# One of four units of a routed layer multiplied without its layer norm, the norm applied to its outputs

## Time and profile before

| what | value |
|---|---|
| median of 3 runs | 748.06 us (747.79 to 748.12) |
| the profiled execution's own time | 747.98 us |
| its span | 745.7 us |
| PE / DVE / ACT / POOL busy | 737.4 / 509.2 / 337.6 / 42.8 us |
| instructions | 10192 |
| DMA | 117.32 MB, mean 157 GB/s |

### The profile page before, as it was taken

One profiled execution on the slowest core, in us unless ns is written; L12 is line 12 of the kernel. 1 busy time (PEld: TensorE's weight loads), 2 busy tenths in 40 slices (PEclk: granted clock), 3 DMA queues, 4 the chain that ended last, 5 costly groups with the idle time before them and its releaser, 6 DMA issues.

```text
span 745.7 us, 10192 instructions
## 1 busy us (share of the span) xinstructions
PE 737.4 (99%) x4269; PEld 611.9 (82%) x4269; DVE 509.2 (68%) x490; ACT 337.6 (45%) x427; POOL 42.8 (6%) x51
## 2 busy tenths in 40 slices
PE   7999999999999999999999999999999999999997
PEld 7988887888888888888788888888888888888885
DVE  6899987876767586379989997664633644355522
ACT  5868874746673325242844364234233241333221
POOL 3302203010302000000000000000000000000000
PEclk9999999999999999999999999999999999999999
DMA  9644872547252543667596721170037003200140
GB/s 358 273 171 170 280 262 94 212 160 261 102 184 99 184 142 113 240 212 254 170 388 189 293 87 74 73 306 1 1 141 286 25 1 142 113 2 0 51 180 3
DMA packets 28077, 117.32 MB, mean 157 GB/s; under 512 B 4160, under 2 KB 4352, under 8 KB 20992
## 3 DMA queue, kind: packets, MB, share of 16 engines
q1 hardware_dynamic: 18784, 99.88, 37.1%
q10 hardware_dynamic: 9248, 16.80, 6.0%
HBM read 95.60 MB, written 37.77 MB: 179 GB/s over the span
## 4 chain that ended last, share of the span: by engine, by line
PE 87%; DVE 8%; DMA 2%; issue 1%; ACT 1%; POOL 0%; SPq 0%; DVEq 0%; ACTq 0%
PE main L939 28%; PE main L941 27%; PE main L940 27%; PE lgp L1002 1%; DMA x5f<-xT 1%; PE lgp L1015 1%; PE spare L1015 1%; DVE x5f L1097 1%; DVE x4f L1097 1%; DVE x2f L1097 1%; DVE x7f L1097 1%; DMA wh6f<-x 1%; PE main L1026 0%; PE lgp L955 0%; DVE x3r L1097 0%
## 5 line engine op out<-in xcount | busy, mean ns | idle before, releaser
L1097 DVE TENSOR_TENSOR s<-s,main 128x512 f32<-128x512 f32 x72 | 48.6, 682 | 71.6 <-PE main L941 71.6
L1097 DVE TENSOR_TENSOR u<-u,main 128x512 f32<-128x512 f32 x36 | 24.5, 684 | 41.9 <-PE main L941 41.9
L793 ACT ACTIVATE u<-u 128x512 f32<-128x512 f32 x32 | 20.0, 631 | 56.7 <-DVE u L1097 56.7
L770 ACT ACTIVATE s<-main 128x512 f32<-128x512 f32 x36 | 20.8, 595 | 53.0 <-PE main L941 22.3
L793 ACT ACTIVATE s<-s 128x512 f32<-128x512 f32 x32 | 20.0, 630 | 52.2 <-DVE s L1097 52.1
L793 ACT ACTIVATE rows<-rows 128x512 f32<-128x512 f32 x16 | 10.1, 632 | 64.1 <-DVE rows L1097 64.1
L1097 DVE TENSOR_TENSOR u<-s,main 128x512 f32<-128x512 f32 x32 | 21.6, 684 | 22.5 <-PE main L941 22.4
L1097 DVE TENSOR_TENSOR rows<-s,main 128x512 f32<-128x512 f32 x16 | 11.0, 688 | 30.2 <-PE main L941 30.2
L723 ACT ACTIVATE rows<-rows,nm 128x1024 f32<-128x1024 f32 x23 | 26.6, 1154 | 0.8
L721 ACT ACTIVATE rows<-rows 128x1024 f32<-128x1024 f32 x24 | 25.2, 1049 | 1.9 <-DMA rows<-x 1.2
L940 PE MATMUL main<-x7r,wh2r 128*128 128x512 f32 x48 | 18.7, 389 | 0.0
(11 more groups left out here) (691 smaller groups left out, 2424.2 us busy)
## 6 DMA issues: line engine op xcount, KB each, us to landing
out<-x SPq DMA_DIRECT2D x31, 512.0 KB, 10.5
rows<-x SPq DMA_DIRECT2D x26, 512.0 KB, 4.4
H_d<-u ACTq DMA_DIRECT2D x32, 256.0 KB, 3.5
H_d<-s ACTq DMA_DIRECT2D x16, 256.0 KB, 4.9
rows<-xh_d SPq DMA_DIRECT2D x16, 256.0 KB, 5.5
w2f<-w2T SPq DMA_DIRECT2D x2, 2048.0 KB, 10.1
wl6f<-wB SPq DMA_DIRECT2D x3, 1024.0 KB, 8.2
wl4f<-wB SPq DMA_DIRECT2D x3, 1024.0 KB, 6.5
```

What stands on the lines that cost most here:

```text
L770: eng.activation(s1[:, j, :], bk, ACT.Copy).then_inc(s_pa, 1)
L793: eng.activation(c, c, ACT.Silu).then_inc(s_sl, 1)
L1097: return eng.tensor_tensor(o, a, b, op)
```

## The change

**Unit 0** now takes batch 1 (`BATCH = (1, 0, 2, 3)`; batch 0 is unit 1, `RAW = 1`) and multiplies it as it is. Its blocks are loaded transposed: a in 4 pieces of 256 KB and c in 2 of 512 KB, each in turn with a piece of its weights. No row is normalized or transposed on PE, and `warm` runs 18 transposes once. The silu of unit 0 is left out, so that its plain outputs go to DRAM; its logits are raw too.

**Row jobs.** 40 jobs go through the two row buffers on ACT (`row_sums`): the rows of units 1, 2, 3, of unit 0, and of w1 (a sum only). They reach into unit 3, and row 11 of before (the fourth job) is ACT's. SP's order within a position is now: load of the row, then `stats_out`, then `stats_back`, then `save`. The saves of the normalized batch for unit 4 move to unit 1's blocks: at (6,1) and (6,3) of unit 0 and (0,2) and (1,0) of unit 1, and three sums of unit 1 and its last low part wait for them.

**Last unit.** The second layer takes the units in the order 1, 2, 3, 0. In unit 8 each block gets `fold` (DVE: mean times the sum of the w1 row, less the value, times the deviation) and `activated` (ACT: silu with scale -1). Its blocks are loaded at (4,0), (4,1), (6,0), (6,1) of unit 7. The logits of unit 0 are put right in unit 4 by six DVE operations ahead of `two_greatest`; PE gives the sums of wr with one matmul.

The core of the diff (much of it left out):

```diff
+BATCH = (1, 0, 2, 3)
+RAW = 1
+SOURCE = {L2: 1, L2 + 1: 2, L2 + 2: 3, L2 + 3: 0}
+FOLDED = tuple(n for n in SOURCE if SOURCE[n] < RAW)
+JOBS = [(u, r) for u in (1, 2, 3, 0) for r in range(KT)] + [("w1", r) for r in range(KT)]
+PIECES = {"a": 4, "c": 2}
...
+        job_at = {at: q for q, at in enumerate(
+            [(0, *at) for at in ((2, 1), (2, 3), (3, 0), (3, 1), (3, 3), (4, 0), (4, 2), (5, 0), (6, 0), (6, 2))]
...
+        turned_at = {(0, 4, 0): 2, (0, 6, 0): 3, (1, 1, 3): 4, (1, 5, 1): 5, (2, 1, 3): 6, (2, 5, 1): 7, (3, 1, 3): 0,
+                     (3, 3, 3): 1}
+        back_at = {(0, 4, 1): (1, 0), (0, 6, 1): (1, 1), (1, 2, 0): (2, 0), (1, 5, 2): (2, 1), (2, 2, 0): (3, 0),
+                   (2, 5, 2): (3, 1)}
+        save_at = {(0, 6, 1): "a", (0, 6, 3): "c", (1, 0, 2): "b", (1, 1, 0): "d"}
...
+            def row(q):
+                if q >= 2:
+                    job_done(on, q - 2)
+                of, r = JOBS[q]
+                r0 = r * P if of == "w1" else BATCH[of] * SEQ + r * P
+                eng.dma_start(job_buf(q), (w1 if of == "w1" else x)[r0:r0 + P, :]).then_inc(s_row[q % 2], 16)
...
-            for r in (0, 1):
-                row(r)
-            for k in (0, 1):
-                first_weights(k)
...
+            for b in "ac":
+                for k in range(PIECES[b]):
+                    first_block(b, k)
+                    first_weights(b, k)
             weights(0, 5, 2, 1)
+            load(0, "b")
+            load(0, "d")
+            eng.dma_start(cst[:, :], small).then_inc(s_cst, 16)
             weights(0, 4, 2, 2)
+            row(0)
+            row(1)
...
+                if (n, p, j) in job_at:
+                    q = job_at[(n, p, j)] + 2
+                    if q < len(JOBS):
+                        row(q)
+                if (n, p, j) in turned_at:
+                    stats_out(turned_at[(n, p, j)])
+                if (n, p, j) in back_at:
+                    stats_back(*back_at[(n, p, j)])
+                if (n, p, j) in save_at:
+                    save(save_at[(n, p, j)])
...
+            def first_product(k):
+                part_in(on, "a", k)
...
+                    ins = three(main[bank[(0, 0, j)]][:, :], wh[:, k, js], wl[:, k, js], xh[:, k, :], xl[:, k, :],
+                                k == 0, False)
...
-            warm(spare, 29)
-            on.wait_ge(s_id, 2)
-            turn(0)
-            turn(1)
-            warm(main[0], 14)
...
+            warm(spare, 18)
+            for k in range(4):
+                first_product(k)
...
                     if at == (1, 3):
                         for b in "acbd":
                             logits(0, b)
+                        on.wait_ge(s_one, 1)
+                        on.wait_ge(s_sw, 1)
+                        eng.matmul(wr_sums, ones, wrs[:, :], start=True, stop=True).then_inc(s_wm, 1)
...
+            def fold(n, b):
+                kh, h = BLK[b]
+                v = xf(n, b)
+                loaded_in(on, n, b)
+                on.wait_ge(s_bc[1], 16 * BACK[1][(n, h)])
+                job_done(on, len(JOBS) - 1)
+                mean, rstd = bcs[1][:, 0, :], bcs[1][:, 1, :].unsqueeze(1).to_broadcast([P, 4, HT])
+                for j in range(4):
+                    o = 4 * kh + j
+                    ins = eng.scalar_tensor_tensor(v[:, j, :], mean, ws[:, o:o + 1], v[:, j, :], ALU.mult, ALU.subtract)
+                link(ins)
+                tt(v, v, rstd, ALU.mult).then_inc(s_fd, 1)
...
+            def logits_normalized():
...
+                for s in range(2 * RAW):
+                    of = L[:, 4 * s:4 * s + 4, :]
+                    mean, rstd = (mvu[:, s, 4 * e:4 * e + 4].unsqueeze(2).to_broadcast([P, 4, E]) for e in range(2))
+                    part_ = rest[:, 4 * s:4 * s + 4, :]
+                    link(tt(part_, mean, wr_sums.unsqueeze(1).to_broadcast([P, 4, E]), ALU.mult))
+                    link(tt(of, of, part_, ALU.subtract))
+                    link(tt(of, of, rstd, ALU.mult))
...
                 if at == (0, 1):
                     x_sum(n, 1)
-                if n < GATE and at == (0, 2):
+                if n == RAW and at == (0, 0):
+                    normalize(n, "b")
+                if RAW <= n < GATE and at == (0, 2):
                     normalize(n, "d")
...
+                        if n == RAW:
+                            on.wait_ge(s_xs[0], 16)
```

More of the change, by code:

```diff
@@ L18 @@
 QC = D // NQ
-BN_ROWS = (11,)
 NU = 4
@@ L256, in program @@
         acc = [lgp[1], spare]
-        s_row = [sem(f"s_row{i}") for i in range(8)]
+        wr_sums = spare[:, 0:E]
+        s_row = [sem(f"s_row{i}") for i in range(2)]
         s_pl = [sem(f"s_pl{i}") for i in range(PLACES)]
@@ L277, in program @@
         s_t = sem("s_t")
-        s_w0 = [sem(f"s_w0{k}") for k in range(4)]
+        s_x0 = {b: [sem(f"s_x0{b}{k}") for k in range(PIECES[b])] for b in "ac"}
+        s_w0 = {b: [sem(f"s_w0{b}{k}") for k in range(PIECES[b])] for b in "ac"}
+        s_xh0 = sem("s_xh0")
+        s_xo0 = sem("s_xo0")
         s_wh0 = sem("s_wh0")
@@ L327, in program, with job_buf, job_loaded, job_done @@
         rows8 = [slice(Q * q, Q * q + E) for q in range(NQ)]
[L329 to L346, removed]
+        def job_buf(q):
+            return rows[:, q % 2, :]
+        def job_loaded(on, q):
+            on.wait_ge(s_row[q % 2], 16 * (q // 2 + 1))
+        def job_done(on, q):
+            on.wait_ge(s_st2, q + 1)
+        def part(v, b, k):
+            m = 4 // PIECES[b]
+            return v[:, k * m:(k + 1) * m, :]
         def xf(n, name):
@@ L559, in _ @@
                     gated((1, 4, 5, 6)[behind[at] // 4], behind[at] % 4)
-                if n and at == (0, 0):
+                if n and n not in FOLDED and at == (0, 0):
                     load(n, "d")
@@ L902, in _ @@
                     high(n, 6)
-                if m < NN:
+                if m in FOLDED:
+                    if at == (5, 0):
+                        activated(m, "a")
+                        high(m, 0)
+                    if at == (5, 2):
+                        activated(m, "c")
+                elif m < NN:
                     if at == (5, 0):
@@ L966, in first_product @@
                     js = slice(j * P, (j + 1) * P)
[L967 to L969 removed]
+                    ins = three(main[bank[(0, 0, j)]][:, :], wh[:, k, js], wl[:, k, js], xh[:, k, :], xl[:, k, :],
+                                k == 0, False)
+                    if k == 3:
                         ins.then_inc(s_mm, 1)
@@ L1239, in w_sum @@
                     if w == 0:
-                        for q in range(4):
-                            on.wait_ge(s_w0[q], 16)
+                        for s in s_w0["a"]:
+                            on.wait_ge(s, 16)
                         on.wait_ge(s_wl[5], wloads[(0, 5)])
@@ L1501, in _ @@
                         logits_turned(2 * n + 1)
-                if n == 1 and at == (0, 0):
-                    normalize(1, "b")
+                if n in FOLDED and at == (0, 0):
+                    fold(n, "d")
                 if n > L2 and at == (0, 1):
@@ L1527, in _ @@
                     low(n, 6)
-                if m < GATE:
+                if m in FOLDED:
+                    if at == (4, 2):
+                        fold(m, "a")
+                    if at == (5, 1):
+                        fold(m, "c")
+                    if at == (6, 2):
+                        fold(m, "b")
+                if RAW < m < GATE:
                     if at == (3, 3):
```

554 lines of the change are left out of this document (200 added, 354 removed).

## The result

| | before | after |
|---|---|---|
| median | 747.94 us (747.79 to 748.12) | 743.53 us (742.52 to 743.81) |
| profiled execution | 747.98 us, span 745.7 | 743.6 us, span 741.8 |

The ratio is 0.9938, 95% interval 0.9921 to 0.9956. The forecast was 739.5 us, so the direction and the range held and the size did not: 4.4 us of gain against 8.6. Repeats of the changed kernel spread over 1.3 us, those of before over 0.3 us.

A forecast was written before the change was run, and what follows sets the result against it. PE was taken to bound the kernel, busy 737.4 of 745.7 us. The terms -6.4 - 6.9 + 2.1 + 1.3 + 1.3 = -8.6 us gave 739.5 us, range 735.0 to 744.0.

The forecast's parts named there:

- Parts 1 and 2: Opening of unit 0: first matmul at 6.0 us, 6.4 us earlier; products 0 and 1 another 6.9 us shorter.
- at most 1 us: Opening: the first matmuls might still run slow after the 18 transposes, a cost of at most 1 us.
- Rival B: Opening fed too late: first w piece +2.3 us, blocks b and d +2; 743.8 us, up to 746; chance 0.12.
- Part 3: SP's queue at (4,0): row load ahead of stats_out delays the statistics; unit 1 starts 2.1 us late, bounds 0 and 3.
- Part 4: Unit 1: saves of a and c ahead of block d's load make product 2 wait, +1.3 us, bounds -0.3 and +4.
- Part 5: Unit 4, product 2: six operations added to a late DVE row cost PE +1.3 us, bounds 0.8 and 2.0.
- Costs at nothing: Last unit's folds (20 us of DVE, 8 us of ACT) and ACT's additional jobs cost PE no time.
- A: Rival: the queue order around unit 1 costs nothing, parts 3 and 4 at nought; 735.7 us; chance 0.13.
- C: Rival: the array stays at 1.2 GHz in the opening; 8.6 us of slow matmuls cancel the gain; chance 0.03.
- D: Rival: another load holds the first product until after 10 us; 743.5 to 748 us; chance 0.02.
- PE's forecast waits: Waits at unit 1's start, its product 2 and unit 4's product 2; PE waits about 4.5 us where it waited 0.8.

The follow-up runs named there:

- e8_feed: Kernel after with SP's order changed: small statistics transfers first, block c's load behind the read-back, save a earlier, save c behind block d's load; 736.43 us.
- e1b_order: Kernel after with stats_out and stats_back issued ahead of the row load at each position of SP's queue; one run, 741.37 us.
- e3_saves: Kernel after with only the saves of blocks a and c of unit 1 issued earlier, at (6,0), SP's order otherwise unchanged; 742.13 us.
- e5_nowarm: Kernel after with 2 instead of 18 identity transposes ahead of the first matmul; 742.37 us.
- e6_router: Kernel after with the six DVE operations on the raw logits moved from unit 4 to position (3,3) of unit 3; 742.18 us.
- e4_warm: Kernel after with 34 identity transposes on PE filling the gap ahead of unit 1; 743.50 us.
- e9_all: e8_feed with the six raw-logit DVE operations and the choice of the two greatest moved from unit 4 to unit 3; 734.82 us.

## Why the prediction was half right

- **Parts 1 and 2, the opening: right.** First matmul at 5.76 us against 6.0, product 3 at 31.66 against 31.7. The sum was 13.3 us, and 13.34 came. In the experiments with `warm` whole product 3 lay between 31.57 and 32.77 us, so the tenth is luck and about 1 us is what the forecast was good for; the slow first matmuls of four of these kernels, up to 0.8 us, are the "at most 1 us" that I had put into the range. Rival B, the opening fed late, falls.
- **Part 3, the failed step: the size of the delay at unit 1.** Mechanism, place and releaser were as forecast, and so was the row load: SP issued it at 67.06, and 80.4 less the 13.34 gained by then is 67.06. What came behind it was mis-sized. "From its end to the read-back 2.3 us" measured 72.45 - 68.95 = 3.5 us, and "lands 4.8 us later" measured 5.5 us. I had taken both durations from rows before which the last large load had gone out 2.45 us earlier (block c at 75.07, the small transfers at 77.52, kernel before), and laid them 0.37 us behind a row load of 512 KB that the change puts there. With it 4.15 us came for 2.1, above my bound of 3. In `e8_feed`, where the row load comes behind and block c too, the read-back goes out 5.0 us earlier and the hole is gone; 3.5 of the 5.0 are the earlier issue, the rest the stores' own time. `e1b_order` separates the two: there too the stores go out at 63.90, but 0.8 us behind the 1 MB load of block c, and the read-back goes out only at 69.29 against 67.48. The Trainium skill (DMA: Bandwidth & Descriptors, Queues, rings and completion order) says that each DMA engine takes the descriptors of a queue in their order. By that rule small transfers pay for what was issued before them, and the trace agrees here: from the stores' last issue to the read-back it took 3.5 us behind the row load, 4.0 behind block c (`e1b_order`) and at most 2.2 with neither right ahead (`e8_feed`). It is not the whole: the second statistics, below, took as long with nothing right ahead.
- **A term left out: the clock after the hole.** I had asked about the clock in the opening alone. A hole of 4.15 us let it fall to 0.50, 2.9 us more for PE, which d's lateness then covered. Waits of 1.2 and 1.65 us left the clock at 1.00 (`e1b_order`; product 2 of unit 4 in the kernel after, where it reads 1.00 from 355 to 362 us). The holes of 3.3 to 4.0 us at the start of unit 1 were each followed by 0.50 (the kernel after, `e3_saves`, `e5_nowarm`, `e6_router`). But the wait of 3.53 us in `e1b_order` was not, and the one of 2.04 us in `e4_warm` was. So the length of a hole alone does not tell whether the clock falls, and the forecast hole of 2.1 us need not have been safe; what decides it stays open.
- **Part 4, block d: mechanism right, size wrong by 4.6 us.** Landing was put at 117.7, which is 104.4 in times of after; it was 108.97. The load went out at 95.36 instead of 92.3, since the second statistics and a held row load came ahead of it, and took 13.6 us, against 12.04 from 105.66 to the forecast landing. Product 2 was forecast at 129.5, or 116.2 in times of after, and came at 120.79, late by the same 4.6 us: this is the term that the path went through. PE's own lateness hid it from the accounts. From the unit's start at 90.76, 26.0 us and the clock's 2.9 put PE at product 2 at 119.7 even with d in time, so the added wait that shows there is only 0.8 us (3.71 less 2.9), under the 1.3 forecast. The two terms also hang together: with the statistics earlier, in `e1b_order`, the load of d goes out 2.3 us sooner. `e1b_order` shows what d costs when PE is early: 3.5 us.
- **Part 5, unit 4: right.** 1.35 us came for 1.3, and 1.36 went with the six operations. The choice of the two greatest, which was already there, held that product up by another 0.45 us (236.31 us in `e9_all` against 236.76).
- **Costs at nothing: right.** No run shows PE waiting for a fold; the folds and ACT's 40 jobs are covered.
- **Rivals.** A was wrong for this kernel, but its 735.7 us is what the change is worth with the queue in order: 736.43. C did not come; its mechanism is real, 1.2 to 2.9 us in the opening with 2 transposes against 0 to 0.8 with 18, far from the 8.6 it needed. D falls.

As a sum: -13.34 forecast and come, +4.30 for +2.1 at unit 1 (the hole, and 0.15 elsewhere in unit 0), +3.71 for +1.3 up to product 2, +1.35 for +1.3. That is -3.98 for -8.6. One number of the prediction does not follow from its own parts: PE's forecast waits, 2.1, 1.6 and 1.7 us, add up to 5.4 us and not to 4.5; nothing else rests on it.

Left open: the second statistics of unit 1. In `e8_feed` they need 4.30 us, in a stretch in which the DMA engines move over 400 GB/s (76 to 86 us), the read-back another 5.93, and DVE waits 4.6 us for it. How much of that is their own queue and how much ACT's stores beside it was not separated, and giving them an earlier place was not tried. The difference of `e5_nowarm` to the kernel after, 1.2 us to the better, is not explained; in its rows d lands at 107.81 and product 2 starts at 120.06, 0.7 us earlier, although the opening is slower.

## What to carry to other kernels

A duration read from a trace belongs to the state of its queue: small transfers that the change puts right behind a large one can take 1.2 us longer than their row (3.5 for 2.3), so list what is issued ahead of them before taking the row. When two chains end at nearly the same place, repairing either gives little (1.55 and 1.4 us here) and both give most of it (6.0 of the 7.1 us that SP's order was worth), so look for the second before judging the first. And put the clock into the price of a wait: waits of 1.0 to 1.65 us cost PE their own length here, one of 2.04 us cost 1.4 us more, four of 3.3 to 4.0 us about 2.9 us more each, and one of 3.53 us nothing more.

## What the hardware showed that was not expected

- Four holes of 3.3 to 4.0 us on PE at the start of unit 1 were each followed by 0.50 of the clock for about 6 us, 13 or 14 matmuls of 512 columns at 0.43 us. A wait of 3.53 us ahead of a block's logits (`e1b_order`) was followed by none, one of 2.04 us at the same place (`e4_warm`) by six.
- Transposes of the identity alone held the clock at 1.00 over 3.6 us. Ahead of the first matmul, 18 of them left none to four matmuls slow, 2 of them 6 or 14.
- In the opening the granted clock reads 1.00 while matmuls start 0.43 us apart; the spacing is what to trust there.
- Four stores of 1 KB needed between 2.2 and 4.0 us from their last issue to the read-back: 3.5 and 4.0 behind a large transfer, but 4.0 also once with none right ahead (the second statistics in `e8_feed`), while the DMA engines moved over 400 GB/s.
